# A two-layer graph transformer on one core: the second graph's steps and the row statistics built inside the combinations, the experts' second bias added by DVE, their scatters tied to PE

## The reference, cut to what matters

```python
xn = _layernorm(x)
x = x + _L0_gnn_ref(xn, edge_index, ...) + _L0_mix_ref(xn[None], ...)[0]      # edge attention
x = x + _L0_ffn_ref(_layernorm(x)[None], ...)[0]                               # 8 experts, top 1
xn = _layernorm(x)
x = x + _L1_gnn_ref(xn, edge_attr_4, edge_attr_10, ..., src, dst) + _L1_mix_ref(xn[None], ...)[0]
x = x + _L1_ffn_ref(_layernorm(x)[None], ..., L1_ffn_edge_index)[0]            # gate over a second graph
```

```python
    hmid = jax.nn.relu(jnp.einsum('ecd,edf->ecf', buf, w1) + b1[:, None, :])
    ybuf = jnp.einsum('ecf,efd->ecd', hmid, w2) + b2[:, None, :]
```

## Time and profile before

| | us |
|---|---|
| runs | 3315.05 median (3310.11, 3315.05, 3315.64) |
| profiled execution, whole | 3317.73 |
| profiled execution, span of the trace | 3315.9 |

### The profile page before, as it was taken

The page is one execution under the profiler, slowest core; times in us unless marked ns, Lnnn a source line. Parts: engine busy times, 40 slices in busy tenths (PEclk is TensorE's granted clock), DMA queues, the critical chain, the costliest instruction groups (busy, mean ns, idle before and its releaser), DMA issues. The chain is left out here.

```text
span 3315.9 us, 40935 instructions
## 1 busy us (share of the span) xinstructions
PE 2403.5 (72%) x11239; PEld 1554.5 (47%) x11240; DVE 2041.8 (62%) x4110; ACT 1368.6 (41%) x3768; POOL 1746.9 (53%) x1762
## 2 busy tenths in 40 slices
PE   0798677777777376789998676777778488888381
PEld 0455455555554265345633332233327377777271
DVE  2544899999998886100045388888884442222568
ACT  0122555565553244311125378788783022222130
POOL 1243767667662075367632477777772147777000
PEclk9899788888888555789978799888889679999685
DMA  5000766667660000333321233333330311111104
GB/s 117 20 32 29 223 198 200 200 194 200 199 188 19 4 2 2 101 102 114 76 59 53 58 92 93 94 97 96 94 87 2 74 21 35 35 35 35 14 1 166
DMA packets 174629, 286.74 MB, mean 86 GB/s; under 512 B 56528, under 2 KB 117213, under 8 KB 174414
## 3 DMA queue, kind: packets, MB, share of 16 engines
q0 software_dynamic: 79568, 187.15, 21.1%
q1 hardware_dynamic: 79444, 74.85, 7.8%
q10 hardware_dynamic: 15402, 22.14, 1.9%
HBM read 247.75 MB, written 36.25 MB: 86 GB/s over the span
## 5 line engine op out<-in xcount | busy, mean ns | idle before, releaser
L2169 POOL DMA_INDIRECT cv_x<-x_tab,e_src x440 | 480.4, 1092 | 195.4 <-issue 89.0
L2182 PE MATMUL cv_ps<-cv_msg,cv_hot 128*128 128x512 f32 x880 | 450.3, 671 | 179.8 <-DVE acc L2232 162.3
L839 POOL DMA_INDIRECT at_kv<-kv_tab,e_src x440 | 463.1, 1053 | 222.6 <-PE at_a L971 106.2
L2182 PEld LDWEIGHTS cv_ps<-cv_msg,cv_hot 128*128 128x128 f32 x880 | 184.6, 216 | 445.2 <-DVE cv_msg L2221 222.7
L1869 POOL DMA_INDIRECT pairs<-gating_pair,gating_place x288 | 280.1, 973 | 205.8 <-issue 88.0
L2568 POOL DMA_INDIRECT gs_h<-h_tab,e_src x312 | 296.7, 951 | 170.7 <-issue 94.8
L2195 ACT ACTIVATE cv_msg<-cv_x,factors 128x64 f32<-128x64 f32 x1320 | 356.6, 333 | 0.0
L2232 DVE TENSOR_TENSOR acc<-acc,cv_ps 128x256 f32 x880 | 297.4, 416 | 2.7 <-DVE acc L2232 2.2
L2193 ACT ACTIVATE cv_msg<-cv_x,factors 128x256 f32<-128x256 f32 x440 | 217.9, 495 | 160.3 <-DMA cv_x<-x_tab,e_src 160.3
L949 PE MATMUL at_q<-q_parts,at_hot_n 128*128 x1320 | 230.1, 330 | 61.6 <-DVE at_kv L1028 52.7
L971 PE MATMUL at_a<-at_kv,at_hot_e 128*128 128x264 f32 x880 | 248.5, 411 | 3.9 <-DVE at_kv L1044 3.9
(11 more groups left out here) (529 smaller groups left out, 4690.4 us busy)
## 6 DMA issues: line engine op xcount, KB each, us to landing
x_w<-in_L_ffn_w SPq DMA_DIRECT2D x16, 1024.0 KB
at_rel_row<-e_rel_rows SPq DMA_DIRECT2D x110, 128.0 KB, 4.3
experts_out<-gs_y ACTq DMA_DIRECT2D x20, 512.0 KB, 2.7
x_y<-experts_out SPq DMA_DIRECT2D x20, 512.0 KB, 5.0
at_kv<-kv_tab,e_src POOLq DMA_INDIRECT x440, 3.8
cv_x<-x_tab,e_src POOLq DMA_INDIRECT x440, 2.8
kv_tab<-p_qkv SPq DMA_DIRECT2D x25, 256.0 KB, 2.0
gs_h<-h_tab,e_src POOLq DMA_INDIRECT x312, 2.4
```

Of the source, the lines that this page charges most:

```text
L839: nc.gpsimd.indirect_dma_start(out=kv[:, t % (RING * Q4), 0:2 * D], out_offset=None, in_=kv_tab, in_offset=bass.IndirectOffsetOnAxis(ap=e. ...
L2169: nc.gpsimd.indirect_dma_start(out=xg[:, i % RT, u, :], out_offset=None, in_=x_tab, in_offset=bass.IndirectOffsetOnAxis(ap=e.src[:, t:t + ...
L2182: nc.tensor.matmul(ps[u][:, :], hot[:, i % 2, u, :], msg[:, i % 2, u, :], start=True, stop=True).then_inc(summed, 1)
```

## The change

Part by part, in the order of the program:

1. `build_steps` becomes the class `Steps` with the pieces `load`, `store` (SP), `widen`, `flip` (PE), `gather` (POOL), `count`, `cuts`, `mark`, `settle` (DVE). `layer_stats` becomes `LayerStats` with `block` (one BN_STATS), `end` and `finish` (the chain, in a block of its own). For the first graph `first_steps` puts the 25 BN_STATS of n0 between `cuts` and `mark`, that is while POOL gathers.
2. `combine0` gets the BN_STATS of n1, one behind each block's last addition; its chain runs right after it. `layer_stats` n2 stays, now as two blocks.
3. In `experts0` L1477 goes. b2 is loaded as 128 copies of its row (128 KB for 1 KB) and DVE adds it while it copies the sum out. For experts 2 to 7 SP waits for DVE before it issues b2. POOL waits, before each scatter, for a mark of PE's progress, 22 scatters per expert.
4. `combine1` takes in the whole build of the second graph's steps and the BN_STATS of n3. The two blocks behind it shrink to n3's chain.
5. `Experts1.load` moves into `gate_rows`: SP issues two loads behind each five stores, and b1 and b2 last.
6. The second graph's tables take the place of buffers that are free by then, and two tiles of `sort_edges` share memory with others.

```diff
+def first_steps(nc, k, pairs, e, stats, got_x):
+                st.count(dve)
+                st.cuts(dve)
+                dve.wait_ge(got_x, 32)
+                for b in range(NB):
+                    stats.block(b)
+                st.mark(dve)
+                st.settle(dve)
+                stats.end(dve)
...
+class LayerStats:
+    def block(self, b):
+        self.nc.vector.bn_stats(self.parts[:, b, :], self.k.X[:, b, :]).then_inc(self.noted, 1)
+    def end(self, dve):
+        dve.wait_ge(self.noted, NB)
...
 def combine0
                         c.link(v.tensor_tensor(xb, xb, ps_o[j][:, 0:D], ALU.add))
+                        stats.block(b)
...
 def experts0
-                        sp.dma_start(b2[:, j, :], a["L0_ffn_b2"][ds(e, 1), :]).then_inc(got[j], 16)
+                        if e >= 2:
+                            sp.wait_ge(y_kept, 2 + (e - 1) * len(TC))
+                        sp.dma_start(b2[:, j, :], wide(a["L0_ffn_b2"][ds(e, 1), :], [P, D])).then_inc(got[j], 16)
+            def pace(n):
+                per = scatter.turns * U // NE
+                e, x = n // per, n % per * 16 // per
+                marks = []
+                if 0 < x <= 8 or e and not x:
+                    marks.append((h_done, e * FC + x))
+                elif x > 8:
+                    marks.append((y_done, e * len(TC) + (x - 8) // 2))
+                return [(sem, count) for sem, count in marks if count > 0]
...
-                        nc.tensor.matmul(ps_y[q % 2][0:n, 0:D], k.ones[0:1, 0:n], b2[:, j, :], start=True, stop=False)
...
-                            v.tensor_copy(y[0:n, j, q, :], ps_y[q % 2][0:n, 0:D]).then_inc(y_kept, 1)
+                            v.tensor_tensor(y[0:n, j, q, :], ps_y[q % 2][0:n, 0:D], b2[0:n, j, :], ALU.add).then_inc(y_kept, 1)
...
 def combine1, POOL
                     nc.gpsimd.tensor_tensor(xb, xb, bias[:, :], ALU.add).then_inc(biased, 1)
+                    if b == 2 * B5 - 1:
+                        st.gather(pool)
...
 def combine1, PE
-                for i in range(0, NB // B5 - 1):
-                    turn(i)
-                turn(NB // B5 - 1, last=True)
+                turn(0)
+                st.widen(pe)
+                turn(1)
+                turn(2)
+                turn(3)
+                st.flip(pe)
+                turn(4, last=True)
...
 def combine1, DVE
+                        if b:
+                            dve.wait_ge(chain, b + 2)
+                            stats.block(b - 1)
                 keep(0, 0)
+                st.count(dve)
+                turn(0)
+                turn(1)
+                st.cuts(dve)
+                turn(2)
+                turn(3)
+                st.mark(dve)
+                turn(4, last=True)
+                st.settle(dve)
                 dve.wait_ge(chain, NB + 2)
+                stats.block(NB - 1)
+                stats.end(dve)
...
 def gate_rows, SP
+                    x1.load(sp, i)
```

More of the change, by code:

```diff
@@ L199, in _ @@
[L199 to L209 removed]
+                st.load(sp)
@@ L211, in _ @@
+                st.store(sp)
             @block.tensor
             def _(pe):
-                pe.wait_ge(cmp_done, 1)
-                nc.tensor.matmul(wide_end[:, 0:chunks], k.ones[0:1, :], end_step[:, :], start=True, stop=True).then_inc(spread, 1)
-                pe.wait_ge(cmp_done, 2)
-                for j, x in enumerate((rel_t, here[:, 1])):
-                    for g in range(groups):
-                        ins = nc.tensor.transpose(turned[j][:, g * P:(g + 1) * P], x[:, g, :], k.ident[:, :])
-                    ins.then_inc(flipped, 1)
+                st.widen(pe)
@@ L421, in _ @@
                 v = nc.vector
-                for i in range(0, NB // B5):
-                    for j in range(B5):
-                        v.bn_stats(parts[:, ds(i * B5 + j, 1), :], k.X[:, ds(i * B5 + j, 1), :]).then_inc(chain, 1)
-                dve.wait_ge(chain, NB)
-                c = Chain(dve, chain, NB)
+                c = Chain(dve, chain)
                 c.link(v.tensor_tensor(t[:, 0], parts[:, :, 1], parts[:, :, 4], ALU.subtract))
@@ L439, in _, with layer_stats @@
                                               op0=ALU.mult, op1=ALU.mult))
+def layer_stats(nc, k, name):
+    with Scope(nc) as s:
+        stats = LayerStats(nc, s, k, name)
+        with nc.Block() as block:
+            @block.vector
+            def _(dve):
+                for b in range(NB):
+                    stats.block(b)
+                stats.end(dve)
+        stats.finish()
 class Loads:
@@ L1859, in __init__, with run @@
         self.sent = [s.sem(name + f"sent{h}") for h in range(2)]
-    def run(self, nc, k, pool, pairs, pair, place_i, placed=None):
+    def run(self, nc, k, pool, pairs, pair, place_i, placed=None, pace=None):
         for i in range(self.turns):
@@ L1868, in run @@
                 c = (self.first + i) * U + u
+                if pace is not None:
+                    for sem, count in pace(i * U + u):
+                        pool.wait_ge(sem, count)
                 nc.gpsimd.indirect_dma_start(
@@ L2979, in dram @@
             return nc.dram_tensor(name, shape, dt, kind="Internal").ap()
-        def steps(e, name, pairs, chunks, groups, n):
-            build_steps(nc, k, name, pairs, chunks, groups, n, e.valid, e.starts, e.ends, e.rel, e.src, e.rel_rows,
-                        e.block_row, e.chunk, e.flags_tab, e.link_tab, e.hole, e.step_row)
         kv_tab, x_tab = dram("kv_tab", [NPAD, 2 * D]), dram("x_tab", [NPAD, D])
@@ L3046, in program @@
[L3046 to L3064 removed]
+                        d_parts = t3.sb("d_parts", [P, NB, 3, H2], BF)
@@ new lines, in program @@
+                        gate_rows(nc, k, h_tab, d_parts, xnT, row_cols, x1)
+                        gate_scores(nc, k, e2, h_tab, d_parts, rows, score, x1, xnT, y_tab)
+                    segment_softmax(nc, k, "m2_", G2, H2, score, e2.valid, e2.starts, e2.ends, 1.0)
+                    gate_sums(nc, k, e2, rows, score, acc, x1, xnT)
+                y = t.sb("x1_y", [P, RING1, NX, D])
+                back = [t.sem(f"x1_back{x}") for x in range(RING1)]
+                top_two(nc, k, acc, row_cols, gates, y, back, y_tab)
@@ L3067 @@
+                experts1(nc, k, x1, y, back, y_tab, gates, out)
 _PLAIN = ["x", "L0_gnn_Wq", "L0_gnn_bq", "L0_gnn_Wk", "L0_gnn_bk", "L0_gnn_Wv", "L0_gnn_bv", "L0_gnn_Ws", "L0_gnn_bs",
```

399 lines of the change are left out of this document (210 added, 189 removed).

## The result

| | before | changed |
|---|---|---|
| median, us (runs) | 3312.58 (3308.87 to 3315.64, 4) | 3257.30 (3256.07 to 3266.17, 4) |
| span of the profiled execution, us | 3315.9 | 3254.3 |

The changed kernel takes 0.9839 of the time of the one before (95% interval 0.9818 to 0.9861): 55.3 us less in the medians, 61.6 between the two profiled executions. The forecast was 51.6 less, 3263.5 us.

The account below looks back on a forecast made before the run. No engine bounds the whole kernel; block by block, DVE bounds `combine0` and PE `experts0`. The terms -8.3 + 0 + 0.6 - 27.0 - 18.4 + 1.5 sum to -51.6 us, giving 3263.5 us, range 3249 to 3284.

Parts of the forecast that it names:

- Opening, n1, n2, gate_rows: Terms for these stages: opening -8.3 us, n1's statistics moved into `combine0` 0, n2 as two blocks +0.6, `gate_rows` +1.5.
- experts0 (a): In `experts0`, dropping the b2 product from PE saves 0.62 us 32 times: -19.8 us, at least -13.8.
- experts0 (b): The wait for expert 7's loads, blamed on the last 16 scatters, goes through `pace`: -9.2 us, or 0.
- experts0 (c): b2's larger load in `experts0` shows as 0.3 us for each of six experts: +2 us (0 to +5).
- the rival in which every load comes too late: In `experts0` every expert loses 9.2 us to a late load: +20 us, 3335 us; chance of slower 0.02.
- experts0 (d): POOL's paced scatters in `experts0` keep up with the experts and land before ACT's last store: no cost.
- The gathers' part: In `combine1`, POOL's biases queue behind nine gathers, so DVE and PE wait: +10.0 us, plus 3.0 for PE's slow clock.
- `mark` and `flip`: In `combine1`, PE waits at `flip` for DVE's `mark`, then does six transposes: +8.5 us, plus 2.5 for the clock.
- the statistics' cover: In `combine1`, n3's statistics of 24 blocks cost nothing, since DVE has 1.4 us of work per block and PE 3.3.
- The load of expert 7: Rival: expert 7's slow load in `experts0` has another cause and stays, total gain 42.4 us, 3272.7 us; chance 0.16.
- the clock in `combine1`: Rival: PE's clock stays down after the first wait, +20 to +35 us; chance 0.09, shared with a dearer `gate_scores` start.
- The cheaper waits: Rival: in `combine1` PE recovers at once and the gathers' wait is shorter, -10 us, 3253 us; chance 0.11.

Follow-up runs that it names:

- n1_own: The changed kernel with n1's row statistics back in a block of their own behind `sort_edges`, on a slower chip: 3830.73 us, ratio 0.9468 to the kernel before.
- a_b2_pe: The changed kernel with the b2 product back on PE and DVE only copying: 3280.57 us.
- b_early16: The kernel before with the last 16 scatters of `experts0` put ahead, beside expert 5's load: 3310.76 us, ratio 0.9985.
- a_free: The changed kernel without the marks that tie the scatters of `experts0` to PE's progress: 3249.84 us, ratio 0.9797.
- c_gather: The changed kernel with the nine gathers in `combine1` issued one behind each of the biases 10 to 18: 3254.15 us.
- c_mark: The changed kernel with `mark` in six pieces ahead of DVE's additions of blocks 17 to 22, and `flip` behind block 23's products: 3253.69 us.
- a_early16: The changed kernel, marks kept, with the last 16 scatters put ahead, eight in expert 4's second half and eight in expert 5's: 3259.22 us, ratio 0.9821.

## Why the prediction was right, point by point

- **Opening, n1, n2, gate_rows**: within 0.7 us each. (The 25 statistics of n0 stood 32 us behind the wait for the gathers, not the 20 that the prediction says; nothing was worked out from it.) The statistics on DVE in `combine0` cost what they save (`n1_own`: 1.0 us between the two), as the earlier trace rows said; the reading of DVE as its bound holds.
- **experts0 (a)**, the product: forecast 19.8; `a_b2_pe` measured 23.3 between the medians and 26.4 from the block's first product to its last. The mechanism was right and the term too small by 4 to 7 us.
- **experts0 (b)**, the stall of 9.2 us: it went, and the guess at its cause stood for expert 7 (`b_early16`), but its size does not follow from the 16 alone. What was wrong is who removes it: not the marks, but already the shorter experts (`a_free`). On a chip like the first, `pace` could have been left out.
- **experts0 (c)**, the wider load of b2: small waits of 0.2 to 1.3 us at single experts, as said; the rival in which every load comes too late did not come true.
- **experts0 (d)** is the step that failed: the last two "go out 3.7 us before PE ends, and land before ACT's last store. Nothing." The last is issued at 1653.47, as PE ends, and the block waits for it until 1664.47, so that the pause at its end is 6.8 us longer. I took the scatters' issue for their landing, and the same 16 whose weight I used in (b) I forgot in (d). That (a) was too small by about as much, and the sum for `experts0` came out at 26.2 for 27.0, was luck.
- **combine1**: both waits stood at their places with their releasers. The gathers' part, forecast 10.0 + 3.0 with the clock, was 12.9; `mark` and `flip`, forecast 8.5 + 2.5, were 9.8. `c_gather` and `c_mark` took away 11.7 and 8.2 of these. The gain of the statistics' cover (24 of 25 free) is as said.
- **return0**, -7.0 us: in thirteen profiles without filler the clock came back 11 to 40 us behind the first product there, in kernels that have the same instructions in it, with no order by their edits; from its start to n2 the stage took 65.3 to 73.6 us. So I count this gain to the execution that was profiled, not to the change.
- **The rivals**: the load of expert 7 was not slow, the clock in `combine1` was back after the first wait within two blocks, no expert missed its load by 3 us. The cheaper waits came true for 1.3 us of their 10. How much of the two waits is the clock (forecast 5.5 us) no run separates.

## What to carry to other kernels

Work moved into a block with an in-order helper engine should be dealt out one piece per round, not in one lump: the nine gathers and the marking cost 19.9 us more in a lump than in pieces, at equal work: `combine1` with all that was put into it then takes 97.7 us, for 93.7 before. A block's end waits for the landing of its last transfers, so small writes must be out 8 to 11 us earlier in this kernel. And a limit on how fast an engine may issue scattered writes can cost 7 us on one chip and save 165 us on another, so judge it on more than one.

## What the runs showed of the hardware that I had not expected

- 128 writes of 8 bytes into one KB, issued every 1.27 us, went with waits of 2.6 to 5.8 us for the load beside them, and the block went on 9.5 to 11.2 us after the issue of the last; beside spread ones the waits were 1.90 us at most, and the block went on after 7.9 us (1662.18 to 1670.04 in `a_early16`).
- One program can differ by 22% between chips: the kernel before took 3316 us on two and 4045 on two others. In the traces taken on the slower ones the time is longer where POOL issues many indirect DMAs (`attention`, `sort_edges`, `gate0`, `experts0`, `convolve`, `gate_scores`); it is the same in the stages without them, and in `route0` and `return0`, which have 25 each.
- On a slower chip, beside free scatters, DVE stood idle for some 44 us at a time with its data in place, PE waited for DVE, and the DMA engines moved 1 GB/s.
- Behind a pause PE's clock stayed at 1.2 GHz for 11 to 40 us of nearly unbroken small products (20 rows, or two columns of weights) in the same code, with no order by the edits; filler products in the pause kept it at 2.4 GHz.
